# Two attention and expert layers on one core: at most two scatters by GpSimd under way

## The reference

```
x = x + attention(context, layernorm(x), mask)             # 8 heads of 32
x = x + experts0(layernorm(x))                             # 8 experts, top 2, inner width 704, and a shared expert of 352
x = x + depool(layernorm(x), context, patch_lens)          # linear layer, scan over the context, gather
x = x + experts1(layernorm(x))                             # 32 experts, top 6, inner width 128, and a shared one of 512

# experts0, per token:  sum over its 2 experts of  p_e * (silu(x Wg_e) * (x Wu_e)) Wd_e
# experts1, per token:  sum over its 6 experts of  w_e * relu(x U_e)^2 D_e
```

## Time and profile before

| | |
|---|---|
| time, median of 3 runs | 889.14 us (884.67 to 889.75) |
| profiled execution, its own time | 888.47 us |
| its span | 886.6 us |
| TensorE busy | 722.6 us, 82% |
| GpSimd busy | 308.5 us, 35% |
| granted TensorE clock, mean | 0.903 |
| moved by all transfers | 181.22 MB |
| of that by GpSimd's queue | 38.68 MB in 13,344 packets |

### The profile page before, as it was taken

How to read it: one execution, slowest core, us unless ns; L and a number is a source line. 1 busy time by engine, 2 the same in 40 slices (tenths; PEclk the granted TensorE clock), 3 DMA queues, 4 the chain that set the end, 5 groups by cost and what they waited for, 6 DMA issues and landing times.

```text
span 886.6 us, 14153 instructions
## 1 busy us (share of the span) xinstructions
PE 722.6 (82%) x4526; PEld 631.4 (71%) x4526; DVE 416.7 (47%) x1615; ACT 273.0 (31%) x620; POOL 308.5 (35%) x322
## 2 busy tenths in 40 slices
PE   3868886389999999999899888866776868787865
PEld 2647776289999999999899877533456757676754
DVE  4998664022333243546644742725104444456563
ACT  2636631022111111222223122321123455445540
POOL 1333307600010111100552354172712656556560
PEclk9898859589999999999999998796978899989998
DMA  8999992231776767755866624242646556587866
GB/s 257 396 296 268 257 252 97 102 125 53 231 231 219 218 221 244 246 169 190 304 218 232 217 89 170 92 166 87 217 154 189 177 158 191 164 288 243 285 215 250
DMA packets 93534, 181.22 MB, mean 204 GB/s; under 512 B 9857, under 2 KB 54998, under 8 KB 93182
## 3 DMA queue, kind: packets, MB, share of 16 engines
q1 hardware_dynamic: 78048, 138.67, 50.9%
q0 software_dynamic: 13344, 38.68, 11.6%
q10 hardware_dynamic: 2046, 2.71, 1.0%
HBM read 134.07 MB, written 65.62 MB: 225 GB/s over the span
## 4 chain that ended last, share of the span: by engine, by line
PE 56%; DVE 16%; issue 10%; another core or an unknown queue 6%; DMA 4%; ACT 3%; POOL 3%; SPq 1%; DVEq 0%; POOLq 0%; ACTq 0%
PE PB L618 16%; PE PB L655 11%; PE PB L632 5%; PE PB L825 4%; PE PB L816 4%; PE PB L763 3%; POOL rows_out L1930 3%; PE PB L777 2%; PE PB L804 2%; DMA X<-in_x 2%; PE PB L684 1%; PE PB L600 1%; DMA MEM<-rows_out 1%; DVE WK L1256 1%
## 5 line engine op out<-in xcount | busy, mean ns | idle before, releaser
L618 PE MATMUL PB<-XT,MEM 128*128 128x128 f32 x1584 | 185.9, 276 | 1.1 <-issue 1.1
L618 PEld LDWEIGHTS PB<-XT,MEM 128*128 128x128 f32 x1584 | 181.7, 193 | 1.5 <-issue 1.3
L1882 POOL DMA_INDIRECT sorted_y<-WK x36 | 34.5, 958 | 279.0 <-DVE WK L1470 279.0
L1891 POOL DMA_INDIRECT rows_in<-MEM x96 | 93.5, 974 | 65.1 <-DVE MEM L1674 36.6
L655 PE MATMUL PB<-MEM,WK 128*128 x432 | 99.7, 380 | 3.3 <-DVE MEM L1646 1.9
L825 PE MATMUL PB<-MEM,WK 128*128 x228 | 67.6, 424 | 32.0 <-DVE WK L1823 26.1
L655 PEld LDWEIGHTS PB<-MEM,WK 128*128 128x128 f32 x432 | 79.3, 190 | 13.2 <-issue 3.9
L1930 POOL DMA_INDIRECT rows_out<-WS,MEM x58 | 56.7, 977 | 64.4 <-ACT WS L1045 49.2
L825 PEld LDWEIGHTS PB<-MEM,WK 128*128 128x128 f32 x228 | 42.2, 207 | 41.2 <-issue 36.9
L1930 POOL DMA_INDIRECT rows_out<-MEM x56 | 56.2, 1003 | 40.5 <-ACT MEM L1045 25.7
L939 ACT ACTIVATE XT<-PB 128x256 f32<-128x256 f32 x52 | 19.8, 381 | 162.2 <-PE PB L600 134.2
(11 more groups left out here) (280 smaller groups left out, 1255.4 us busy)
## 6 DMA issues: line engine op xcount, KB each, us to landing
MEM<-in_w SPq DMA_DIRECT2D x36, 896.0 KB
rows_in<-in_consts SPq DMA_DIRECT2D x32, 600.0 KB, 12.2
MEM<-in_w SPq DMA_DIRECT2D x36, 512.0 KB
MEM<-rows_in SPq DMA_DIRECT2D x58, 300.0 KB
MEM<-rows_out SPq DMA_DIRECT2D x16, 768.0 KB, 7.0
MEM<-in_w SPq DMA_DIRECT2D x32, 256.0 KB, 2.8
MEM<-in_w SPq DMA_DIRECT2D x2, 3072.0 KB, 18.9
sorted_x<-MEM SPq DMA_DIRECT2D x1, 5070.0 KB, 39.7
```

Source lines behind the costliest of these rows:

```text
L618: t = e.matmul(o[:, to:to + P], UPW[m][i % (3 - m)][:, k, c * P:(c + 1) * P], XT[:, n % 2, k, :], start=(k == 0), stop=(k == 1))
L1882: e.indirect_dma_start(out=DY, out_offset=bass.IndirectOffsetOnAxis(ap=DEST[:, i:i + 1], axis=0), in_=YS[:, i % 2, :], in_offset=None).the ...
L1891: e.indirect_dma_start(out=DX1, out_offset=bass.IndirectOffsetOnAxis(ap=SLOT1[:, i, j:j + 1], axis=0), in_=XR[:, i, :], in_offset=None).th ...
```

## The change

Ahead of every scatter of the sorted rows, the routed rows and the results, GpSimd waits for the landing of the last but one scatter of the same kind. The semaphores are named anew to match: `sent0` and `sent1` by the index of the expert choice, `rows0` and `rows1` by its parity (before there was one semaphore per group of tiles), and SyncE's fetches wait for the last of each. The results have 16 semaphores in turn already. No instruction changes its place in any engine's stream, and no transfer, buffer or size changes.

```diff
--- before.py
+++ after.py
@@ -1870,9 +1870,10 @@
             q.wait_ge("zeroed")
             for i in range(NT):
                 for k in range(2):
+                    q.wait_ge(f"sent{k}", i - 1)
                     e.indirect_dma_start(
                         out=DX, out_offset=bass.IndirectOffsetOnAxis(ap=SLOT[:, k, i:i + 1], axis=0),
-                        in_=XNA[:, i, :], in_offset=None).then_inc(*q.land(f"sent{i // 4}", i, k))
+                        in_=XNA[:, i, :], in_offset=None).then_inc(*q.land(f"sent{k}", i))
 
             def scatter(n, nb):
                 kind, i = item(n, nb)
@@ -1888,9 +1889,11 @@
                 q.wait_ge("clear", 31)
                 for r in range(lo, hi):
                     i, j = GB[g] + r // TOPK, r % TOPK
+                    if i or j > 1:
+                        q.wait_ge(f"rows{j % 2}", i if j > 1 else i - 1, (j - 2) % TOPK)
                     e.indirect_dma_start(
                         out=DX1, out_offset=bass.IndirectOffsetOnAxis(ap=SLOT1[:, i, j:j + 1], axis=0),
-                        in_=XR[:, i, :], in_offset=None).then_inc(*q.land(f"rows{g}", i, j))
+                        in_=XR[:, i, :], in_offset=None).then_inc(*q.land(f"rows{j % 2}", i, j))
 
             def block_iteration(n, nb):
                 scatter(n, nb)
@@ -1927,6 +1930,7 @@
                     q.wait_ge("by", r)
                     q.wait_ge("mq", r // 2)
                     for b in (2 * r, 2 * r + 1):
+                        q.wait_ge(f"yb{(b - 2) % 16}", b - 2)
                         e.indirect_dma_start(
                             out=DY1, out_offset=bass.IndirectOffsetOnAxis(ap=DST[:, b:b + 1], axis=0),
                             in_=YB[b // 8 % 2][:, b % 8, :], in_offset=None).then_inc(*q.land(f"yb{b % 16}", b))
@@ -1972,8 +1976,8 @@
             def fetch(n, nb):
                 kind, i = item(n, nb)
                 if kind == "b":
-                    for g in range(NG):
-                        q.wait_ge(f"sent{g}", 4 * g + 3, 1)
+                    for k in range(2):
+                        q.wait_ge(f"sent{k}", NT - 1)
                     q.wait_ge("tab")
                     if i >= 3:
                         q.wait_ge("tx", n - 3)
@@ -2058,8 +2062,8 @@
             def fetch1(s):
                 a = 2 * s % 12
                 q.wait_ge("wi", NR - 1, 1)
-                for g in range(NR):
-                    q.wait_ge(f"rows{g}", GB[g + 1] - 1, TOPK - 1)
+                for j in range(2):
+                    q.wait_ge(f"rows{j}", NT - 1, TOPK - 2 + j)
                 q.wait_ge("bt", s - 6)
                 q.wait_ge("mq", (s - 6) // 2)
                 e.dma_start(XB[:, a:a + 2, :],
```

## The result

The changed kernel takes 908.41 us in the median of 4 runs (903.17 to 912.63), the kernel before, on the same chip, 889.44 us (884.67 to 892.49): a ratio of 1.0204, 95% interval 1.0154 to 1.0255. The forecast was 910 us. The sum came out right; two of its terms did not, by 36 us each, in opposite directions.

What follows compares the result with a forecast made beforehand. TensorE at 82% busy, held during back-to-back scatters, and GpSimd near the bound in the results; 2 + 2 + 6 - 3 + 15 = +22 us on 888.47, taken as +21, forecast 910 us, range 855 to 942.

Steps and rivals of the forecast that it cites:

- Do the holds go away?: Step on TensorE's idle stretches during back-to-back scatters: release needs a 2.26 us pause, so the 148 and 582 us holds stay.
- The first rival: Holds go: the cap's few tenths free TensorE, 49 us in three stretches fall away, 861 us; chance 0.22.
- Sorted rows: The 32 sorted scatters, 134.77 to 174.35 us: 2.60 us landings per pair instead of 2.53, on TensorE's path, +2 us.
- Routed rows: Groups 0 and 1 among the blocks, +2 us (0 to 12); groups 2 and 3, delaying the results, +6 (2 to 20).
- Results: Result scatters at one landing a pair: first part 96 us against 99, -3; second 102 against 87, +15.
- Nothing happens: Rival: a capped queue lands scatters faster, landings near 2.6 us, results stay at 3.2 a pair, 890 us; chance 0.18.
- The cap is the bound everywhere: Rival: landings of 3.6 us in the first results part, 4.4 in the second; +67, 955 us; chance 0.17.
- What would show it: Signs in the profile after: sorted run 40.5 to 43 us, TensorE idle about 20 us from 150, results 3.2 and 3.8 a pair.

Runs made afterwards that it cites:

- the parts: Against the kernel before, the wait for the last but one landing on one kind alone: sorted rows 0.9811, routed rows 0.9842, results 1.0392.

## Why the prediction was right, and where it wasn't

**Right by its number and its sign, and that by luck: two errors cancelled.** The forecast was +10 us up to the first result and +12 in the results; measured are -26.4 and +48.1, and -3.4 at the end.

- *"Do the holds go away?"* This step failed. I read in the earlier trace rows that TensorE is released 2.26 us after GpSimd's last start with 1.8 scatters in flight, and made of it that only a pause as long as 2.26 us could release it. The row is ScalarE's, and the sorted rows of the same trace say otherwise. There TensorE goes on one matmul at a time after the last scatter's start at 174.35, and even after SyncE has seen the landing at 176.95, and is free at 179.99, 5.6 us behind the last start and 3.0 behind the landing:

```profile
174.37 0.37 PE L632 MATMUL PB<-XT,WS 128*96 128x128 f32 x1 [2.42 <-issue]
176.47 0.37 PE L632 MATMUL PB<-XT,WS 128*96 128x128 f32 x1 [1.73 <-issue]
178.57 0.37 PE L632 MATMUL PB<-XT,WS 128*96 128x128 f32 x1 [1.73 <-issue]
```

  The end of a run tells how long the hold takes to drain after a run at full rate; it doesn't tell how much slower the run must be for nothing to pile up. Measured: the cap's 0.15 us more per scatter frees about half of the stretch, a pause of 0.45 all of it. The first rival had this ("the few tenths that the cap adds free TensorE"), with the condition that it decides once the 148 us hold is gone. Its 49 us were too many as a sum; the gains of the parts are 17 and 14 us by the ratios 0.9811 and 0.9842.
- *Sorted rows, "+2 us (1 to 4), TensorE is held until the run ends"*: the run got 5.3 us longer (44.85 for 39.58), more than the 2.60 us landing gives, since the next start follows 2.7 to 2.9 us behind the one it waits for, and not 2.60, and near two gaps of 2.5 and 2.7 us 3.7 to 4.2. With TensorE free this isn't on the path any more: the first block came 13.4 us sooner behind the first scatter.
- *Routed rows, "+2" and "+6 us"*: GpSimd does wait for its queue, 78.8 us in all. The +6 charged the run's length to the first result, while TensorE's own delay stood in that place before. With the hold gone the run became the bound, and starting the results 14.2 us behind it is still earlier.
- *Results, "-3" and "+15"*: right mechanism, wrong size, and +48.1 us lies outside the bounds that I gave (-3 to +29). In the first part 27 and a half pairs take 104.0 us, 3.8 a pair for 3.2 forecast; in the second 29 take 129.2, 4.45 for 3.76. The mistake is in the landings: I added 0.4 us to the last packets of scatters that went out in the kernel before, and weighted loaded and unloaded times by the share of the loads. With the cap every landing is on the path, those of 6.3 to 6.6 us too, and my upper bound took 4.4. With 16 buffers ahead I also counted on TensorE to run on; it can't for long, when the stage's rate is the landing.
- *"Nothing happens"*: with three under way in the sorted rows it nearly holds (0.9948), with two it doesn't. The figure of the Trainium skill ("DMA: Bandwidth & Descriptors", section "Anatomy of one DMA - SWDGE (gpsimd) path": 2.0 us and the bytes), from which I estimated 2.3, is near the landing of the last sorted scatter after the change, 178.67 to SyncE's fetch at 181.18, 2.51 us. Under load, at 6.3 to 6.6 us, it is out by nearly a factor of three.
- *"The cap is the bound everywhere"* came true in the results alone: 4.1 a pair instead of 3.2.
- *What would show it*: of the signs I named, the 32 sorted scatters took 44.85 us and not 40.5 to 43, and TensorE was idle for 12 us and not 20 from 148 on. Both pointed to the first rival.

**What stays open.** What TensorE waits for isn't in the profile; it is called "issue", "remote" or an unknown queue. The Trainium skill, "SBUF — State Buffer", section "Who interferes with whom", has it that TensorE never waits for another engine at the SBUF ports. No run here can show whether that is so. Two things fit with something that fills up when scatters start faster than it empties: more time between the starts is enough (at one per 1.71 us there is no hold, at 1.49 there is), and at full rate the hold outlasts the last sorted scatter's start by 5.0 to 5.8 us in each of six profiles, and after the change by 0.8. This is argued and not shown; what fills up isn't known. Open is also why the cap frees more than a pause of the same mean, and the last per cent: the parts multiply to 0.9811 x 0.9842 x 1.0392 = 1.0034, and the full change has 1.0204, measured on another chip. Results without waits take 189 to 193 us on the chips of the experiments and 185.0 on that of the change, with the wait 234.3 and 233.1; so the wait's price there is 3 to 7 us higher, of the 15 us that 1.7% are; the rest isn't explained.

## What to carry to other kernels

A cap on transfers under way does two things, and each wants its own price: it spaces the starts, which may free another engine, and it makes the issuer's rate that of a landing. Put it where the run isn't itself the bound (here the sorted and routed rows: 3.5% faster), and leave it out, or set it so wide that a loaded landing fits in, where the stage lives by the issuer's rate (here 2 under way cost 4%, and 3 or 4 little or nothing). Price each place by itself: a sum that comes out right says nothing of its terms. When one engine is idle for no reason that the profile shows while another issues back to back, try a few tenths of a microsecond between the issues before anything else, and vary the dose: 0.08 us between most starts (0.18 in the mean) showed nothing in the time here, 0.45 gave 2%.

## What the runs showed of the hardware

- GpSimd's scatters of 128 rows (48 packets each) hold TensorE when they start every 1.26 us: 49 matmuls in 34 us. At 1.44 in the mean there are 53, at 1.49 110, at 1.71 263, and with the cap of two, at 1.41 to 1.43, 108 to 150. The hold sets in some scatters after the run's start: in 134 to 146 us TensorE was busy 10.9 of 12 us in the kernel before too.
- With TensorE held its granted clock is low: 0.63 of full speed in that window before, 0.75 to 0.97 with the cap, 1.00 with the longest pauses. The same matmuls are slower as well, 0.47 us each for 0.23 (eight of line 777 at 3.78 us behind the hold, 1.89 later).
- The hold outlasts the scatters: in the kernel before, TensorE is free 5.6 us after the last start and 3.0 us after its landing was seen.
- A landing is no constant: 2.5 us with nothing else on the queues, 6.3 to 6.6 us beside 768 KB loads of results.
- A clear of 64x8 costs nothing between two scatters (1.27 us from start to start with it, 1.26 without), since it falls into the 0.30 us that are there anyway; four small ones cost 0.08 us between most starts.
